# Attention on one core: the products that find the row maxima contract 32 rows instead of 96, two key blocks at once, and the score banks go by head

## The chip, the cores and the metric

The kernel runs on one core of a Trainium2 chip. The metric is the device time of one execution in microseconds (us); the fastest of repeated executions and their median lie close together. TensorE is the engine of the matrix products, VectorE (DVE), ScalarE (ACT) and GpSimd (POOL) work on elements, and SyncE (SP) issues the transfers that matter here. Products land in PSUM, which has 8 banks of 512 f32 numbers in each of 128 partitions.

## The reference

The program is two layers on 4096 tokens of 256 numbers (a gated delta rule with a mixture of experts, then a linear attention and a softmax attention, added). The change lies in the softmax attention alone, which has 8 heads of 32 numbers and no mask:

```python
attn = jnp.einsum('bhqd,bhkd->bhqk', q, k) * scale
attn = jax.nn.softmax(attn, axis=-1)
attn_out = jnp.einsum('bhqk,bhkd->bhqd', attn, v)
```

Softmax is the same whatever number is subtracted from all scores of a query. The kernel subtracts a maximum so that the exponentials stay in range; that maximum need not be exact.

## The kernel before

`phase_attention` is the last part of the program. Queries come in NB = 8 blocks of 512, heads in HP = 4 pairs, keys in NKT = 32 tiles of 128. One step is one key tile j for one pair p of one block b; n = 4b + p counts the pairs, and a pair has 32 steps. Everything is written out in order by hand and tied by semaphores.

Queries and keys are held as two f16 parts, high and low. `queries` has the high part in rows 0 to 31, the high part again in rows 32 to 63 and the low part in rows 64 to 95; `keys` has high, low, high. One product over these ROW = 96 rows gives high x high + high x low + low x high. Row 96 of the queries holds minus the maximum, and row 96 of the keys a constant, so that a product over KR = 97 rows gives the score less the maximum.

TensorE's order in a step is: the scores of tile j for both heads (L2127, four products of 64 key rows by 512 queries into `p_s[j % 2]`, two banks, one per head); then two maximum steps for a later pair (L2063, two products each, 64 queries by a block of 512 keys, into `p_m[k % 2]`, one bank); then the values of tile j-1 (L2082, f32, 64 columns for each head, into `p_o`). A product has a stationary side of 64 columns, so two products with outputs in partitions 0 to 63 and 64 to 127 use different columns of the array. An f32 product appears as two records.

The other engines follow. ScalarE takes the exponential of both heads in one instruction of 1024 elements (L2203) into `prob`, two deep. VectorE reduces each maximum bank of 512 to one column of `part_max` (L2221); 64 of them (NMAX = 2 heads x 4 query tiles x 8 key blocks) make a pair's maxima. `max_end` joins them, `max_rows` (L2072, eight small products with one column each) turns them into rows, and ScalarE copies these into row 96 of the queries (`copy_rows`, L2186). At step 1 ScalarE also copies the numerators of the pair before (`take_nums`, L2195), after VectorE has copied `p_o` (L2235). SyncE issues the query loads of the next block once a pair's scores are done. Ahead of the first step the 64 maximum steps of pair 0 and the first EARLY = 6 of pair 1 (12 products) run with nothing beside them.

The waits that the change touches are: the scores of step j wait for the exponentials of step j-2 (`exp_d`), the values of j-1 for those of j-1, a maximum product for the reduction two before it (`red_d`), and an activation for the scores of its step (`s_d`) and the values of step j-2 (`pv_d`).

Of the kernel before, what the change touches and what calls it, by code (L numbers as in the profile page):

```python
# [19 lines left out]
BLK = 512  # L20
# [19 lines left out]
DF = D // HF  # L40
# [3 lines left out]
SCORE_SCALE = D ** -0.5 / QK_SCALE ** 2  # L44
# [1807 lines left out]
def phase_attention(nc, g, ctx):  # L1852
# [5 lines left out]
    def sb(name, shape, dt=F32):  # L1858
        return ctx.enter_context(nc.sbuf_tensor(name, shape, dt))
# [3 lines left out]
    def sem(name):  # L1863
# [3 lines left out]
    HP = HF // 2  # L1867
    NKT = T // P
    KB = T // BLK
# [25 lines left out]
    part_max = sb("part_max", [P, 2 * SUB, KB])  # L1895
# [23 lines left out]

# [8 lines left out]
    LOADS = 6  # L1928
    READY = 3 * NB + sum(D >> (b * EX // NB) < D for b in range(NB)) + 2 * KC
    g.used_sems = sems  # L1930

# [7 lines left out]
        with looped(nc, engine, NB - 1) as i:  # L1939
            one(i + 1, i)  # L1940

    def max_steps(j):

        start = EARLY + 2 * j if j < MAX_END else 2 * (j - MAX_END)
        return range(start, start + 2)

    def max_step(k):

        hh, rest = divmod(k, NMAX // 2)
        return (hh,) + divmod(rest, KB)  # L1950

    block = ctx.enter_context(nc.Block())

    @block.sync
    def _(sp):
        def load_queries(b, p):
            for hh in range(2):
                c, at = place(2 * p + hh)
                for n, part in enumerate((0, 0, 1)):
                    sp.dma_start(queries[n * DF:(n + 1) * DF, p, hh, :],  # L1960
                                 g.parts_d[part * 2 * KC + c, at:at + DF, bass.ds(b * BLK, BLK)]).then_inc(q_in[p], 16)

        for p in range(HP):
            load_queries(0, p)
            for h in (2 * p, 2 * p + 1):
                c, at = place(h)
                for n, part in enumerate((0, 1, 0)):
                    sp.dma_start(keys[n * DF:(n + 1) * DF, h, :], g.parts_d[part * 2 * KC + KC + c, at:at + DF, 0:T]).then_inc(keys_in[p], 16)  # L1968
            if p == 0:
                for dst, src in ((lin_o[:], g.given["lin_o_t"].rearrange("(c p) n -> p c n", p=P)),  # L1970
                                 (nest_o[:], g.given["nest_o_t"].rearrange("(c p) n -> p c n", p=P)),
                                 (bias[:], g.given["lin_o_b"].partition_broadcast(P)), (nest_b[:], g.given["nest_o_b"].partition_broadcast(P))):
                    sp.dma_start(dst, src).then_inc(w_in, 16)

        def store(b):
            sp.wait_ge(out_d, b * SUB + SUB)
            sp.dma_start(g.out[bass.ds(b * BLK, BLK), :].rearrange("(s p) d -> p s d", p=P), out[:]).then_inc(out_out, 16)

        def one(b, before):

            sp.wait_ge(nums_d, b * KC)
            sp.dma_start(lin_q[:], g.lin_q_d[:, :, bass.ds(b * BLK, BLK)].rearrange("c p t -> p c t")).then_inc(lq_in, 16)
            for p in range(HP):

                sp.wait_ge(s_d, (b * HP + p + 1) * NKT)
# [66 lines left out]
    def _(pe):  # L2052
        te = nc.tensor

        def max_product(n, p, k):

            hh, sub, kb = max_step(k)

            if k >= 2 or not isinstance(n, int) or n > 0:
                pe.wait_ge(red_d, n * NMAX + (k - 1))  # L2060
            for x in range(2):
                at = sub * P + x * HALF
                last = te.matmul(p_m[k % 2][x * HALF:(x + 1) * HALF, :], queries[0:ROW, p, hh, at:at + HALF],  # L2063
                                 keys[0:ROW, 2 * p + hh, kb * BLK:(kb + 1) * BLK], start=True, stop=True)
            last.then_inc(mm_d, 1)

        def max_rows(n):
# [6 lines left out]
            last.then_inc(row_d, 1)  # L2074

        def values(n, p, j, hh):
            if hh == 0:
                if j == 0:

                    pe.wait_ge(o_d, n)  # L2080
# [18 lines left out]
            last.then_inc(fin_d, 1)  # L2099


        pe.wait_ge(q_in[0], 16 * LOADS)
        pe.wait_ge(keys_in[0], 16 * LOADS)
        for k in range(NMAX):
            max_product(0, 0, k)

        pe.wait_ge(cleared, 3)
        max_rows(0)
        pe.wait_ge(q_in[1], 16 * LOADS)
        pe.wait_ge(keys_in[1], 16 * LOADS)  # L2110
        for k in range(EARLY):
            max_product(1, 1, k)

        def one(b, before):
            for p in range(HP):
# [3 lines left out]

                pe.wait_ge(rowc_d, n * 2 + 2)  # L2120
                for j in range(NKT):

                    pe.wait_ge(exp_d, n * NKT + (j - 1) if before is not None or p > 0 or j > 0 else 0)
                    for hh in range(2):
                        for x in range(2):
                            at = j * P + x * HALF
                            last = te.matmul(p_s[j % 2][x * HALF:(x + 1) * HALF, hh, :], keys[0:KR, 2 * p + hh, at:at + HALF], queries[0:KR, p, hh, :],  # L2127
                                             start=True, stop=True)
                    last.then_inc(s_d, 1)
                    if j == MAX_END:  # L2130

                        pe.wait_ge(keys_in[nxt2], 16 * LOADS)
                        pe.wait_ge(q_in[nxt2], (b + 1) * (16 * LOADS) if p < HP - 2 else (b + 2) * (16 * LOADS))
# [46 lines left out]
    def _(act):  # L2180
# [16 lines left out]
        def one(b, before):  # L2197
            for p in range(HP):
                n = b * HP + p
                for j in range(NKT):  # L2200
                    act.wait_ge(pv_d, n * NKT + (j - 1) if before is not None or p > 0 or j > 0 else 0)
                    act.wait_ge(s_d, n * NKT + (j + 1))
                    a.activation(prob[:, j % 2], p_s[j % 2][:], ACT.Exp, scale=SCORE_SCALE).then_inc(exp_d, 1)  # L2203
                    if j == 1 and p > 0:
                        take_nums(b * HP + (p - 1))
                    elif j == 1 and before is not None:
                        take_nums(before * HP + (HP - 1))
                    if j == NKT - 2:
                        copy_rows(n + 1, (p + 1) % HP)
# [5 lines left out]
    def _(dve):  # L2215
        v = nc.vector

        def max_reduce(n, k):
            hh, sub, kb = max_step(k)
# [35 lines left out]
        def one(b, before):  # L2255
            for p in range(HP):
# [8 lines left out]
                for j in range(NKT):  # L2265
                    if j == MAX_END:
                        max_end(n + 1)
                    for k in max_steps(j):
                        max_reduce(n + 1 if j < MAX_END else n + 2, k)
# [165 lines left out]
```

## Time and profile before

| what | value |
|---|---|
| time, median of 3 | 4649.83 us (4649.33 to 4651.19) |
| span of the profiled execution | 4658.0 us |
| TensorE busy | 4395.0 us, 94% |
| VectorE busy | 3292.1 us, 71% |
| ScalarE busy | 1913.2 us, 41% |
| GpSimd busy | 1037.3 us, 22% |
| mean granted TensorE clock | 0.980 |

The profiled execution has no time of its own beside its span; the span is 8.2 us above the median of the timed runs. The first 2.69 ms are the other parts of the program, which the change leaves alone. In the profile "PE" is TensorE's products and "PEld" its loads of the stationary side. A product's duration contains the time in which it runs through the array, so that products started 0.22 us apart each last 0.38 us; what a product costs the stream is read from start to start.

### The profile page before, as it was taken

The numbers are of one execution on the slowest core, as the hardware profiler recorded it, in microseconds if no ns is written. First come the engines' busy times: TensorE is split into PE (matmuls) and PEld (weight loads), VectorE is DVE, ScalarE is ACT, GpSimd is POOL, SyncE is SP. The second block draws the span as 40 slices with busy tenths as digits, with TensorE's granted clock in tenths as the row PEclk, the third lists the DMA queues.
The fourth block names the chain that finished last, engine by engine and source line by source line (L and its number), as shares of the span: only waits on it lengthen the run. The fifth ranks groups of instructions, "written<-read, shape, count | busy, mean of one in ns | idle before, by whom it ended". The sixth has DMA issues, their size and how long they took to land. (4 is left out here: it accounts for less than half of the span.)

```text
span 4658.0 us, 151584 instructions
## 1 busy us (share of the span) xinstructions
PE 4395.0 (94%) x64527; PEld 2839.4 (61%) x64527; DVE 3292.1 (71%) x5448; ACT 1913.2 (41%) x2685; POOL 1037.3 (22%) x1042
## 2 busy tenths in 40 slices
PE   5999699999999999999968789999999999999998
PEld 4444499999999999996756624444444444444443
DVE  4899755655655655653459778787878888887876
ACT  2888411111111111110434426565655556565654
POOL 1000143343344344341047630000000000000000
PEclk9999899999999999999989979999999999999999
DMA  4544411111111111112344330000000000000000
GB/s 140 157 130 132 130 56 57 52 53 54 53 55 54 52 56 54 53 47 68 115 124 110 98 72 9 9 14 9 14 9 14 9 14 9 14 9 14 9 14 9
DMA packets 261652, 250.13 MB, mean 54 GB/s; under 512 B 51712, under 2 KB 230016, under 8 KB 260256
## 3 DMA queue, kind: packets, MB, share of 16 engines
q1 hardware_dynamic: 240528, 209.39, 15.0%
q0 software_dynamic: 6144, 16.79, 1.1%
q10 hardware_dynamic: 14352, 14.55, 0.9%
q8 instruction: 520, 8.52, 0.8%
q14 instruction: 108, 0.88, 0.1%
HBM read 135.27 MB, written 105.38 MB: 52 GB/s over the span
## 5 line engine op out<-in xcount | busy, mean ns | idle before, releaser
L2221 DVE TENSOR_REDUCE part_max<-p_m 128x1 f32<-128x512 f32 x2118 | 1364.1, 686 | 378.7 <-PE p_m L2063 371.2
L2203 ACT ACTIVATE prob<-p_s 128x1024 f32<-128x1024 f32 x1024 | 1047.8, 1023 | 749.2 <-PE p_s L2127 747.2
L2082 PE MATMUL p_o<-prob,v_one 128*64 128x512 f32 x4096 | 1054.4, 593 | 3.9 <-ACT prob L2203 0.5
L2063 PE MATMUL p_m<-keys,queries 96*64 96x512 f16 x4236 | 660.9, 387 | 27.9 <-DMA keys<-parts_d 20.3
L2127 PE MATMUL p_s<-queries,keys 97*64 97x512 f16 x4096 | 618.5, 380 | 0.0
L2127 PEld LDWEIGHTS p_s<-queries,keys 97*64 97x64 f16 x4096 | 227.1, 109 | 600.1 <-issue 594.6
L2063 PEld LDWEIGHTS p_m<-keys,queries 96*64 96x64 f16 x4236 | 238.2, 108 | 311.6 <-DVE part_max L2221 56.4
L848 PE MATMUL pd_pre<-inv,step 64*64 64x64 f32 x10240 | 384.4, 219 | 23.8 <-issue 22.1
L2031 POOL TENSOR_TENSOR attn<-o_num,o_inv 32x512 f32<-32x512 f32 x64 | 80.9, 1264 | 1458.5 <-DVE o_inv L2240 1452.0
L2082 PEld LDWEIGHTS p_o<-prob,v_one 128*64 128x64 f32 x4096 | 286.7, 136 | 163.7 <-issue 15.9
L848 PEld LDWEIGHTS pd_pre<-inv,step 64*64 64x64 f32 x10240 | 345.4, 135 | 57.4 <-issue 55.4
L590 PE MATMUL p_proj<-xn_t_all,proj_w_sb 128*128 128x512 f32 x768 | 337.7, 596 | 7.7 <-PEq L2366 7.7
L887 PE MATMUL pd_low<-step,inv 64*64 64x64 f32 x8192 | 304.6, 218 | 6.3 <-issue 3.4
L848 PE MATMUL pd_pre<-inv_low,upper 64*64 64x64 f32 x8192 | 295.0, 219 | 5.5 <-issue 5.5
L1087 DVE TENSOR_TENSOR step<-pd_pre,const 128x512 f32<-128x512 f32 x320 | 215.1, 688 | 105.9 <-PE pd_pre L848 105.9
L887 PEld LDWEIGHTS pd_low<-step,inv 64*64 64x64 f32 x8192 | 278.5, 135 | 10.3 <-issue 6.9
L848 PEld LDWEIGHTS pd_pre<-inv_low,upper 64*64 64x64 f32 x8192 | 273.1, 135 | 9.1 <-issue 6.9
L1091 DVE TENSOR_TENSOR inv_low<-low,pd_low 128x512 f32<-128x512 f32 x256 | 175.9, 687 | 132.8 <-PE pd_low L887 132.8
L590 PEld LDWEIGHTS p_proj<-xn_t_all,proj_w_sb 128*128 128x128 f32 x768 | 146.8, 191 | 193.0 <-issue 187.7
L1101 DVE TENSOR_TENSOR inv<-inv,pd_pre 128x512 f32<-128x512 f32 x256 | 176.1, 688 | 111.3 <-PE pd_pre L848 105.7
L1014 ACT ACTIVATE o_t<-pd_a 128x512 f32<-128x512 f32 x64 | 38.2, 597 | 494.6 <-PE pd_a L913 494.6
L999 ACT ACTIVATE rel<-diff 128x512 f32<-128x512 f32 x64 | 40.4, 631 | 467.4 <-DVE diff L1055 467.4
(245 smaller groups left out, 6612.8 us busy)
## 6 DMA issues: line engine op xcount, KB each, us to landing
q_d<-conv_q SPq DMA_DIRECT2D x16, 1024.0 KB, 5.0
v_d<-conv_v SPq DMA_DIRECT2D x16, 1024.0 KB, 5.0
k_d<-conv_k SPq DMA_DIRECT2D x16, 1024.0 KB, 6.5
sums<-sums_d SPq DMA_DIRECT2D x128, 128.0 KB, 3.0
k_t<-k_d SPq DMA_DIRECT2D x32, 512.0 KB, 4.6
q_t<-q_d SPq DMA_DIRECT2D x32, 512.0 KB, 3.4
v_t<-v_d SPq DMA_DIRECT2D x32, 512.0 KB, 3.4
slots_d<-zero ACTq DMA_DIRECT2D x1, 10112.0 KB, 32.5
```

The costliest lines, as they stand in the source:

```text
L590: last = te.matmul(p_proj[u % RING][:], g.proj_w_sb[:, n, c, p * P:(p + 1) * P], g.xn_t[:, c, b * BLK:(b + 1) * BLK], start=c == 0, stop=c ...
L848: last = te.matmul(out[hs, p, :], lhs(p, hs), rhs(p, hs), start=True, stop=True)
L887: last = te.matmul(p_low[x][hs, p, :], inv[x][hs, p, :], step[x][hs, p, :], start=k == 1 and p == 0, stop=k == NL - 1, skip_group_check=True)
L1087: v.tensor_tensor(step[x][:], p_pre[x][:], over_pairs(masks[:, k - 1, :]), ALU.mult).then_inc(step_d[x], 1)
L1091: v.tensor_tensor(inv_low[x][:], low_1[x][:], p_low[x][:], ALU.add).then_inc(lowc_d[x], 1)
L1101: v.tensor_tensor(inv[x][:] if k < NL else inv_fin[:, n.ring[x]], inv[x][:], p_pre[x][:], ALU.add).then_inc(up_d[x], 1)
L2031: po.tensor_tensor(attn[at:at + DF, c, :], o_num[DEN[hh], :], o_inv[DEN[hh], :], ALU.mult).then_inc(attn_d, 1)
L2063: last = te.matmul(p_m[k % 2][x * HALF:(x + 1) * HALF, :], queries[0:ROW, p, hh, at:at + HALF], keys[0:ROW, 2 * p + hh, kb * BLK:(kb + 1) ...
L2082: product = te.matmul(p_o[64 * hh:64 * hh + VW, :], g.v_one[:, j, p, hh:hh + 2, :].rearrange("p a d -> p (a d)"), prob[:, j % 2, hh, :], s ...
L2127: last = te.matmul(p_s[j % 2][x * HALF:(x + 1) * HALF, hh, :], keys[0:KR, 2 * p + hh, at:at + HALF], queries[0:KR, p, hh, :], start=True, ...
L2203: a.activation(prob[:, j % 2], p_s[j % 2][:], ACT.Exp, scale=SCORE_SCALE).then_inc(exp_d, 1)
L2221: v.tensor_reduce(part_max[:, hh * SUB + sub, kb:kb + 1], p_m[k % 2][:], AX.X, ALU.max).then_inc(red_d, 1)
```

## The change

The maximum products contract only the 32 high x high rows. The upper one reads rows 0 to 31 of `queries` and `keys`, the lower one rows 64 to 95 of `keys` (which hold the high part too) and of a new tile `queries_low`, whose rows 64 to 95 are loaded with the high part of the queries. In one step they take two key blocks of the same head and query tile, into the two banks of `p_m[k % 2]`. So there are NMAX = 32 maximum steps a pair, one in each step, four products each: two row groups by two halves of the columns. VectorE reduces the 1024 elements of both banks in one instruction.

The banks are shared out anew: `p_m` has two pairs of banks in place of two banks, and `p_s` two banks in place of two pairs, one for each head. So the scores of a head at step j wait for that head's exponential at step j-1. ScalarE has one activation of 512 elements for each head and step, and the counts of `s_d` and `exp_d` double. The two bias tiles move into `out`, to make room for `queries_low`.

```diff
-    NMAX = 2 * SUB * KB
+    NMAX = SUB * KB
     MAX_END = NKT - 3
-    EARLY = NMAX - 2 * MAX_END
+    EARLY = NMAX - MAX_END
+    UPPER = slice(0, DF)
+    LOWER = slice(2 * DF, 3 * DF)
...
+    queries_low = sb("queries_low", [P, HP, 2, BLK], F16)
...
-    bias = sb("bias", [P, D])
-    nest_b = sb("nest_b", [P, D])
...
-    p_s = [ctx.enter_context(nc.psum_tensor(f"p_s{n}", [P, 2, BLK], F32)) for n in range(2)]
-    p_m = [ctx.enter_context(nc.psum_tensor(f"p_m{n}", [P, BLK], F32)) for n in range(2)]
+    bias, nest_b = out[:, 0, :], out[:, 1, :]
+    p_s = [ctx.enter_context(nc.psum_tensor(f"p_s{n}", [P, BLK], F32)) for n in range(2)]
+    p_m = [ctx.enter_context(nc.psum_tensor(f"p_m{n}", [P, 2, BLK], F32)) for n in range(2)]
...
+                sp.dma_start(queries_low[LOWER, p, hh, :], g.parts_d[c, at:at + DF, bass.ds(b * BLK, BLK)]).then_inc(q_in[p], 16)
...
-                last = te.matmul(p_m[k % 2][x * HALF:(x + 1) * HALF, :], queries[0:ROW, p, hh, at:at + HALF],
-                                 keys[0:ROW, 2 * p + hh, kb * BLK:(kb + 1) * BLK], start=True, stop=True)
+                for half, (rows, side) in enumerate(((UPPER, queries), (LOWER, queries_low))):
+                    first = (2 * kb + half) * BLK
+                    last = te.matmul(p_m[k % 2][x * HALF:(x + 1) * HALF, half, :], side[rows, p, hh, at:at + HALF],
+                                     keys[rows, 2 * p + hh, first:first + BLK], start=True, stop=True)
...
-                pe.wait_ge(exp_d, n * NKT + (j + 1))
+            if hh == 0 and j == 0:
+                pe.wait_ge(o_d, n)
+            pe.wait_ge(exp_d, n * (2 * NKT) + (2 * j + hh + 1))
...
-                    pe.wait_ge(exp_d, n * NKT + (j - 1) if before is not None or p > 0 or j > 0 else 0)
                     for hh in range(2):
+                        if before is not None or p > 0 or j > 0:
+                            pe.wait_ge(exp_d, n * (2 * NKT) + (2 * j + hh - 1))
                         for x in range(2):
                             at = j * P + x * HALF
-                            last = te.matmul(p_s[j % 2][x * HALF:(x + 1) * HALF, hh, :], keys[0:KR, 2 * p + hh, at:at + HALF], queries[0:KR, p, hh, :],
+                            last = te.matmul(p_s[hh][x * HALF:(x + 1) * HALF, :], keys[0:KR, 2 * p + hh, at:at + HALF], queries[0:KR, p, hh, :],
                                              start=True, stop=True)
-                    last.then_inc(s_d, 1)
+                        last.then_inc(s_d, 1)
...
-                    for k in max_steps(j):
-                        max_product(n + 1 if j < MAX_END else n + 2, nxt if j < MAX_END else nxt2, k)
+                    max_products(n + 1 if j < MAX_END else n + 2, nxt if j < MAX_END else nxt2, max_step(j))
...
-                    act.wait_ge(s_d, n * NKT + (j + 1))
-                    a.activation(prob[:, j % 2], p_s[j % 2][:], ACT.Exp, scale=SCORE_SCALE).then_inc(exp_d, 1)
+                    for hh in range(2):
+                        act.wait_ge(s_d, n * (2 * NKT) + (2 * j + hh + 1))
+                        a.activation(prob[:, j % 2, hh], p_s[hh][:], ACT.Exp, scale=SCORE_SCALE).then_inc(exp_d, 1)
...
-            v.tensor_reduce(part_max[:, hh * SUB + sub, kb:kb + 1], p_m[k % 2][:], AX.X, ALU.max).then_inc(red_d, 1)
+            v.tensor_reduce(part_max[:, hh * SUB + sub, kb:kb + 1], p_m[k % 2][:].rearrange("p h t -> p (h t)"), AX.X, ALU.max).then_inc(red_d, 1)
```

On TensorE, a step in the middle of a pair and the scores of the next, before (`64x512` is the output; the number behind a name is that of the buffer):

```order
L2127 MATMUL p_s0<-queries,keys 64x512 x4
L2063 MATMUL p_m0<-keys,queries 64x512 x2
L2063 MATMUL p_m1<-keys,queries 64x512 x2
L2082 MATMUL p_o<-prob,v_one 64x512 x2
L2127 MATMUL p_s1<-queries,keys 64x512 x4
```

And the same place in the change:

```order
L2130 MATMUL p_s0<-queries,keys 64x512 x2
L2130 MATMUL p_s1<-queries,keys 64x512 x2
L2068 MATMUL p_m1<-keys,queries 64x512
L2068 MATMUL p_m1<-keys,queries_low 64x512
L2068 MATMUL p_m1<-keys,queries 64x512
L2068 MATMUL p_m1<-keys,queries_low 64x512
L2085 MATMUL p_o<-prob,v_one 64x512 x2
L2130 MATMUL p_s0<-queries,keys 64x512 x2
L2130 MATMUL p_s1<-queries,keys 64x512 x2
```

The number of products in a step is the same, 10. Between scores and values there now stand four maximum products with the same output buffer, alternately from `queries` and `queries_low`, and a step writes both score buffers where it wrote one.

On ScalarE, the end of a pair, where the row copies (`queries<-p_f`) stand, before:

```order
L2203 ACTIVATE prob<-p_s1 128x1024
L2203 ACTIVATE prob<-p_s0 128x1024
L2186 ACTIVATE queries<-p_f 1x512 x2
L2203 ACTIVATE prob<-p_s1 128x1024
L2203 ACTIVATE prob<-p_s0 128x1024
L2203 ACTIVATE prob<-p_s1 128x1024
L2195 ACTIVATE o_num<-o_raw 32x512 x2
```

And now:

```order
L2206 ACTIVATE prob<-p_s0 128x512
L2206 ACTIVATE prob<-p_s1 128x512
L2206 ACTIVATE prob<-p_s0 128x512
L2206 ACTIVATE prob<-p_s1 128x512
L2188 ACTIVATE queries<-p_f 1x512 x2
L2206 ACTIVATE prob<-p_s0 128x512
L2206 ACTIVATE prob<-p_s1 128x512
L2206 ACTIVATE prob<-p_s0 128x512
L2206 ACTIVATE prob<-p_s1 128x512
L2206 ACTIVATE prob<-p_s0 128x512
L2206 ACTIVATE prob<-p_s1 128x512
L2197 ACTIVATE o_num<-o_raw 32x512 x2
```

Each activation has become two, one per head; the two copies stand at the same place, now between the activations of step 30 and those of step 31, with two instructions of half the size for each step.

## Rows read from the trace of the kernel before

**Rows 1.** The page: busy time and share of each engine; chain by line.

```profile
PE 4395.0 (94%) x64527; PEld 2839.4 (61%) x64527; DVE 3292.1 (71%) x5448; ACT 1913.2 (41%) x2685; POOL 1037.3 (22%) x1042
...
PE p_o L2082 19%; PE p_m L2063 10%; PE p_s L2127 10%; DVE part_max L2221 1%; PE p_f L2095 1%; PE p_f L2097 1%; PE p_f L2157 0%; PE p_f L2162 0%; PE p_f L2072 0%; DMA keys<-parts_d 0%; DVE o_inv L2240 0%; SPq L1960 0%; SPq L1968 0%; DVE out_tile L2247 0%; ACT prob L2203 0%
```

**Rows 2.** One plain head pair: stretch, us, busy PE, PEld, DVE, ACT, POOL, clock, DMA.

```profile
3563.14:3619.18 56.04, 55.92 (x394) 24.15 (x392) 49.08 (x84) 35.18 (x37) 2.52 (x2) 1.00 0.02 5
```

**Rows 3.** The chain that ended last, one step: start us, us, what.

```profile
3504.26 0.86 PE p_o L2082 x4
3505.12 0.43 PE p_s L2127 x4
3505.55 0.43 PE p_m L2063 x4
```

**Rows 4.** Waits of the attention: who waited for whom, total us, times, longest.

```profile
ACT prob L2203 <- PE p_s L2127: 712.6, 897, 2.8
...
PEld p_m L2063 <- DVE part_max L2221: 14.5, 65, 0.5
```

**Rows 5.** Groups of instructions of the attention: busy us, mean ns of one, idle before.

```profile
L2221 DVE TENSOR_REDUCE part_max<-p_m 128x1 f32<-128x512 f32 x1962 | 1263.6, 686 | 333.2 <-PE p_m L2063 330.2
...
L2203 ACT ACTIVATE prob<-p_s 128x1024 f32<-128x1024 f32 x981 | 1003.8, 1023 | 714.5 <-PE p_s L2127 712.6
...
L2227 DVE TENSOR_REDUCE row_max<-part_max 128x8 f32<-128x64 f32 x31 | 6.8, 220 | 3.2
```

**Rows 6.** TensorE's timeline in the delta stage: start us, us, line, shapes, count.

```profile
1428.15 1.15 PE L848 MATMUL pd_pre<-inv,step 64*64 64x64 f32 x32
1429.23 0.44 PE L926 MATMUL pd_b<-wo,o_t 128*64 128x256 f32 x2
...
1430.80 0.39 PE L926 MATMUL pd_b<-wo,o_t 128*64 128x256 f32 x2
1431.11 1.15 PE L848 MATMUL pd_pre<-inv,step 64*64 64x64 f32 x32
1432.09 0.28 PE L848 MATMUL pd_pre<-k_t 64*64 64x64 f32 x4
```

**Rows 7.** TensorE's timeline at the end of a head pair.

```profile
3506.25 0.59 PE L2082 MATMUL p_o<-prob,v_one 128*64 128x512 f32 x2
3506.78 0.40 PE L2072 MATMUL p_f<-eye_h,neg_max 128*1 128x128 f16 x8
3507.11 0.41 PE L2127 MATMUL p_s<-queries,keys 97*64 97x512 f16 x2
...
3507.34 0.38 PE L2127 MATMUL p_s<-queries,keys 97*64 97x512 f16 x2
```

**Rows 8.** ScalarE: timeline at the end of a pair; a 128x512 activation elsewhere.

```profile
3507.23 1.20 ACT L2186 ACTIVATE queries<-p_f 1x512 f16<-1x512 f32 x2 [0.61 <-PE p_f L2072]
3508.46 1.02 ACT L2203 ACTIVATE prob<-p_s 128x1024 f32<-128x1024 f32 x1
...
L1014 ACT ACTIVATE o_t<-pd_a x64: 597/597/598, 593.7 to 2148.8; 128x512 f32<-128x512 f32 x64
```

**Rows 9.** TensorE's timeline in the second step of a pair.

```profile
3511.02 0.60 PE L2063 MATMUL p_m<-keys,queries 96*64 96x512 f16 x4
3511.73 0.65 PE L2082 MATMUL p_o<-prob,v_one 128*64 128x512 f32 x2
```

**Rows 10.** Timeline ahead of the first step: TensorE, then the DMA queue's issues.

```profile
2694.03 1.24 PE L2063 MATMUL p_m<-keys,queries 96*64 96x512 f16 x4 [0.19 <-DVE part_max L2221]
2695.45 0.64 PE L2063 MATMUL p_m<-keys,queries 96*64 96x512 f16 x2 [0.19 <-DVE part_max L2221]
...
2735.72 1.06 PE L2063 MATMUL p_m<-keys,queries 96*64 96x512 f16 x4
...
2739.60 0.64 PE L2127 MATMUL p_s<-queries,keys 97*64 97x512 f16 x2
...
2694.95 2.27 SPq L1960 DMA_DIRECT2D queries<-parts_d  x5
```

More of the change, by code:

```diff
@@ L1892, in phase_attention @@
     queries = sb("queries", [P, HP, 2, BLK], F16)
+    queries_low = sb("queries_low", [P, HP, 2, BLK], F16)
     eye_h = sb("eye_h", [P, P], F16)
     prob = sb("prob", [P, 2, 2, BLK])
-    part_max = sb("part_max", [P, 2 * SUB, KB])
+    part_max = sb("part_max", [P, 2 * SUB, KB // 2])
     row_max = sb("row_max", [P, 2 * SUB])
@@ L1927, in phase_attention @@
         sem(n) for n in ("lq_in", "base_in", "dens", "dene", "denr", "nums", "lin", "fin", "bb", "out", "out_out"))
-    LOADS = 6
+    KEY_LOADS = 6
+    QUERY_LOADS = 8
     READY = 3 * NB + sum(D >> (b * EX // NB) < D for b in range(NB)) + 2 * KC
@@ L1940, in blocks, with max_step, max_place @@
             one(i + 1, i)
[L1942 to L1947, printed above, removed]
+    def max_step(j):
+        return EARLY + j if j < MAX_END else j - MAX_END
+    def max_place(k):
         hh, rest = divmod(k, NMAX // 2)
-        return (hh,) + divmod(rest, KB)
+        return (hh,) + divmod(rest, KB // 2)
     block = ctx.enter_context(nc.Block())
@@ L1971, in _ @@
                                  (nest_o[:], g.given["nest_o_t"].rearrange("(c p) n -> p c n", p=P)),
-                                 (bias[:], g.given["lin_o_b"].partition_broadcast(P)), (nest_b[:], g.given["nest_o_b"].partition_broadcast(P))):
+                                 (bias, g.given["lin_o_b"].partition_broadcast(P)), (nest_b, g.given["nest_o_b"].partition_broadcast(P))):
                     sp.dma_start(dst, src).then_inc(w_in, 16)
@@ L1983, in one @@
             for p in range(HP):
-                sp.wait_ge(s_d, (b * HP + p + 1) * NKT)
+                sp.wait_ge(s_d, (b * HP + p + 1) * (2 * NKT))
                 load_queries(b + 1, p)
@@ L2053, in _, with max_products @@
         te = nc.tensor
-        def max_product(n, p, k):
-            hh, sub, kb = max_step(k)
+        def max_products(n, p, k):
+            hh, sub, kb = max_place(k)
             if k >= 2 or not isinstance(n, int) or n > 0:
@@ L2099, in final @@
             last.then_inc(fin_d, 1)
-        pe.wait_ge(q_in[0], 16 * LOADS)
-        pe.wait_ge(keys_in[0], 16 * LOADS)
+        pe.wait_ge(q_in[0], 16 * QUERY_LOADS)
+        pe.wait_ge(keys_in[0], 16 * KEY_LOADS)
         for k in range(NMAX):
-            max_product(0, 0, k)
+            max_products(0, 0, k)
         pe.wait_ge(cleared, 3)
         max_rows(0)
-        pe.wait_ge(q_in[1], 16 * LOADS)
-        pe.wait_ge(keys_in[1], 16 * LOADS)
+        pe.wait_ge(q_in[1], 16 * QUERY_LOADS)
+        pe.wait_ge(keys_in[1], 16 * KEY_LOADS)
         for k in range(EARLY):
-            max_product(1, 1, k)
+            max_products(1, 1, k)
         def one(b, before):
@@ L2121, in one @@
                 for j in range(NKT):
-                    pe.wait_ge(exp_d, n * NKT + (j - 1) if before is not None or p > 0 or j > 0 else 0)
                     for hh in range(2):
+                        if before is not None or p > 0 or j > 0:
+                            pe.wait_ge(exp_d, n * (2 * NKT) + (2 * j + hh - 1))
                         for x in range(2):
                             at = j * P + x * HALF
-                            last = te.matmul(p_s[j % 2][x * HALF:(x + 1) * HALF, hh, :], keys[0:KR, 2 * p + hh, at:at + HALF], queries[0:KR, p, hh, :],
+                            last = te.matmul(p_s[hh][x * HALF:(x + 1) * HALF, :], keys[0:KR, 2 * p + hh, at:at + HALF], queries[0:KR, p, hh, :],
                                              start=True, stop=True)
-                    last.then_inc(s_d, 1)
+                        last.then_inc(s_d, 1)
                     if j == MAX_END:
-                        pe.wait_ge(keys_in[nxt2], 16 * LOADS)
-                        pe.wait_ge(q_in[nxt2], (b + 1) * (16 * LOADS) if p < HP - 2 else (b + 2) * (16 * LOADS))
-                    for k in max_steps(j):
-                        max_product(n + 1 if j < MAX_END else n + 2, nxt if j < MAX_END else nxt2, k)
+                        pe.wait_ge(keys_in[nxt2], 16 * KEY_LOADS)
+                        pe.wait_ge(q_in[nxt2], (b + 1) * (16 * QUERY_LOADS) if p < HP - 2 else (b + 2) * (16 * QUERY_LOADS))
+                    max_products(n + 1 if j < MAX_END else n + 2, nxt if j < MAX_END else nxt2, max_step(j))
                     for hh in range(2):
@@ L2218, in max_reduce @@
         def max_reduce(n, k):
-            hh, sub, kb = max_step(k)
+            hh, sub, kb = max_place(k)
             dve.wait_ge(mm_d, n * NMAX + (k + 1))
-            v.tensor_reduce(part_max[:, hh * SUB + sub, kb:kb + 1], p_m[k % 2][:], AX.X, ALU.max).then_inc(red_d, 1)
+            v.tensor_reduce(part_max[:, hh * SUB + sub, kb:kb + 1], p_m[k % 2][:].rearrange("p h t -> p (h t)"), AX.X, ALU.max).then_inc(red_d, 1)
         def max_end(n):
@@ L2267, in one @@
                         max_end(n + 1)
-                    for k in max_steps(j):
-                        max_reduce(n + 1 if j < MAX_END else n + 2, k)
+                    max_reduce(n + 1 if j < MAX_END else n + 2, max_step(j))
                     if done is not None and j == 0:
```

3 lines of the change are left out of this document (removed).

## The prediction

> **What bounds the kernel now.** I read the page first. TensorE is busy for 94% of the span, and the chain that ended last has 19% in the value products (L2082), 10% in the maximum products (L2063) and 10% in the score products (L2127), nearly nothing on another engine [rows 1]. The change touches the attention alone, from about 2693 us on. It has 1024 steps (8 blocks x 4 head pairs x 32 key tiles); one plain head pair takes 56.04 us at a granted clock of 1.00 (2.4 GHz), in which VectorE is busy 49.08 and ScalarE 35.18 [rows 2]. In the chain a step is 0.43 us of scores, 0.43 of maximum products and 0.86 of values: 1.73 in all, without a gap [rows 3]. 32 x 1.73 is 55.3; the other 0.7 us of a pair are the row products (L2072) at the end and one wait on a VectorE copy. Who waits for whom agrees: ScalarE waits 712.6 us for scores, and TensorE's loads wait 14.5 us in all for the maximum reductions [rows 4]. So a step is worth what TensorE's own stream is worth; VectorE and ScalarE have room.
>
> **The change, part by part.**
>
> *Streaming.* Before, the four maximum products of a step are two couples; the halves of a couple lie in different columns of the array and run together, 0.216 us for 512 columns, so 0.43. Now the four lie in four separate pieces of 32 rows x 64 columns. If all four run together they stream for 0.216. That two products in different rows and columns run together is seen in the delta stage: 32 products of 64x64 take 0.98 us, 31 ns each, where a product of 64 columns in two passes streams 53 ns (an eighth of the 0.216 of 512, times two passes) [rows 6]. That two row groups over the *same* columns run together no row shows. Bounds: 0.216 saved, or nothing. I take 0.216: the outputs are in different banks, and nothing in the rows ties a product to its column neighbours. Per step: -0.216.
>
> *Changing the shape of the pieces.* This is the cost that the diff does not name. Scores (97 rows) and values (128) use the whole height of the array; the new products use a quarter of it. The trace has such changes. In the delta stage a batch of 32 64x64 products takes 0.98 us to the next batch of the same shape, and 1.08 to products of 128x64 [rows 6]: 0.10 lost. The first couple after a change also lasts 0.44 against 0.39 for a later one [rows 6], 0.05, as its weights could not be loaded ahead. The reverse change, from products at 1430.80 to 1431.11, is 0.31 where a couple takes 0.216: 0.10 again. In the attention the row products show the same with f16: values at 3506.25 stream 0.43, the next starts at 3506.78, 0.10 late; and the first scores after it last 0.41, the next 0.38, so the load costs 0.02-0.03 with f16 weights [rows 7]. Now each step has two such changes: scores to maximum products (0.095 + 0.024, and 0.012 for four starts), and back to values (0.095 + 0.051, f32 weights). Sum +0.277 a step. With the streaming: +0.061 a step, step 1.79, x 1024 = **+62 us**.
>
> The Trainium skill (TensorEngine Tiling, Key Properties) states that changing the tiling mode, not just the tile, drains TensorE; by that alone the gap would be expected here, and the trace agrees with its 0.10 us at every such change.
>
> *Activations.* One of 1024 elements (1023 ns) becomes two of 512; the same shape on ScalarE takes 597 ns elsewhere [rows 5, 8]. So 1.20 us a step, under 1.79. But the score banks are now one per head, and scores of step j+1 wait for the activation of step j, not j-1. A signal takes some 0.05: the row products end at 3507.18, the copy starts at 3507.23 [rows 7, 8]. Timed from a step's first score, whose product lasts 0.38, the first head's activation ends at 0.43 + 0.60 = 1.03, the second's at 1.63; the second head's next scores may start at 1.68 and are due at 1.79 + 0.22 = 2.01. Slack 0.33: no wait in a plain step. Cover is gone where ScalarE has something else in its queue, twice a pair. (a) At the end of a pair it copies two rows, 1.20 us, starting 0.12 after the step's scores, and activations begin 1.35 after them [rows 7, 8]. Before, the double banks hide this. Now activations end at 1.95 and 2.55; scores due at 1.79 start at 2.00 (0.21 late), those then due at 2.22 start at 2.60 (0.38 late). What is queued behind them on TensorE, the maximum products and values, moves with them. (b) After step 1 it copies the numerators, two instructions again: about 0.1 late, as the steps before have built up slack. Against it, the values of step 1 wait 0.28 for VectorE's copy of the output (0.71 from products to values where 0.43 is usual [rows 9]); with a longer step and a shorter reduction ahead of that copy I make it 0.2, so -0.1. Net +0.6 a pair, x 32 = **+19 us**.
>
> *Reductions.* 512 elements take 686 ns, 64 take 220 [rows 5]: 1.04 ns an element, so 1024 take 1.22 us. A step has one in place of two (2 x 0.686, less a little overlap). VectorE gets lighter; it held TensorE for almost nothing in the steps, so nothing is won there.
>
> *Before the first step.* 64 reductions with TensorE waiting for each go at 1.42 per two [rows 10], 45.5 us; 32 of 1.24 are 39.7: -5.8. The 12 products ahead of the first step take 3.88 [rows 10]; three double ones need some 2.6: -1.3. Two more query loads stand ahead of the keys on the queue, at 2.27 / 5 = 0.45 us each [rows 10]: +0.9. Together **-6 us**. Later query loads are two more per pair, issued a full block ahead of use: nothing. The bias tiles that move into the output tile are read before its first write: nothing.
>
> **The sum**: +62 + 19 - 6 = +75 us on the profiled span of 4658.0, and the same difference on the median of 4649.83, which is 8 us lower: **4725 us**, slower by 1.6%. (0.2%, 9 us, is about what a measurement here tells from no change.)
>
> **Rivals.**
> - *Faster: no gap between shapes.* If the change between whole-height and 32-row pieces cost nothing (the rows show other pairs of shapes, never this one), a step would be 1.51. The waits on ScalarE would grow to about 1.3 us a pair more than before, as its slack shrinks to 0.05: -0.216 x 1024 + 42 - 6 = -186, 4464 us. Against it stands that every change seen, in rows or in columns, costs 0.10. It decides at 0.19: if both changes with their loads cost less than that a step, instead of 0.277, the kernel is faster. 5%. The Trainium skill (TensorE: Matmul & The Clock Gate, Measured speedup vs the span model) has row-packed products starting about 4 ns apart and four at 3.07 times the speed; applied alone to this kernel it would be this rival, but it says nothing there of products of another shape in between.
> - *Half of it*: one of the two changes is hidden, as the 32-row weights load beside the scores. Step 1.727 - 0.216 + 0.146 = 1.657; with waits of some +25 us, 4650 - 72 + 25 - 6, about 4597. 5%.
> - *The row groups run one after the other* (one port for what streams in, or the same columns collide). Then the gaps come and nothing is saved: 0.216 x 1024 more, less the ScalarE waits that the longer step covers (17): 4927 us. Nothing in the trace speaks for or against it but the diagonal pieces of [rows 6]. 9%.
> - *A chain over ScalarE in every step*: activation or semaphores take longer than I have, and the single bank per head becomes the bound. Each 0.1 beyond the 0.33 of slack is 102 us: near 4820. The 597 ns speaks against it. 5%.
> - *No change of time*, where gaps and streaming just cancel: 2%.
> - My forecast: 74%, with its own range 4695 to 4755 (gap 0.09 to 0.11, load 0.02 to 0.06, stalls a pair 0.2 to 1.1).
>
> **Numbers.** Slower by over 0.2%: 74 + 9 + 5 = 88%. Faster: 10%. Same: 2%. The range goes from 4670 to 4800: it holds the likeliest case whole and reaches some way to the ScalarE chain; it leaves out the serial row groups, both faster rivals and the tail of the rest, a little under 2 in 10.
>
> **What would show it.** In the changed trace: four maximum products within some 20 ns of each other; a start 0.31 after the last couple of scores and values about 0.35 after the first maximum product; step 1.79 by the chain; clock still 1.00; a plain pair near 58.5 us; longer steps at the turn of a pair, where TensorE's loads wait for the activation. It is wrong if the step is 1.51 (no gap), 1.66 (one gap) or 2.0 (serial), or if the loads of scores wait for ScalarE in every step.

## The result, and the profile after

The changed kernel takes 4703.77 us (4700.84 to 4710.49) against 4650.51 us (4649.33 to 4652.89): the ratio is 1.0113, with a 95% interval of 1.0101 to 1.0125. It is slower by 53 us, where 75 were forecast, and the time lies in the range.

The page of the profile after, TensorE's share and the chain by line; they answer to [rows 1]:

```profile
PE 4430.8 (94%) x64527; PEld 2637.8 (56%) x64527; DVE 3232.6 (69%) x4389; ACT 1976.6 (42%) x3709; POOL 1037.1 (22%) x1042
...
PE p_o L2085 21%; PE p_s L2130 9%; PE p_m L2068 7%; DVE part_max L2224 1%; PE p_f L2098 1%; ACT prob L2206 1%; PE p_f L2100 1%; DVE o_raw L2238 0%; PE p_f L2159 0%; PE p_f L2164 0%; ACT queries L2188 0%; PE p_f L2077 0%; DMA keys<-parts_d 0%; SPq L1962 0%; SPq L1971 0%
```

TensorE is as busy as before, 94% of a longer span; the maximum products have fallen from 10% of the chain to 7% and the values have risen from 19% to 21%, although no value product was changed. One plain head pair of the profile after (stretch, its length, then busy time of TensorE's products and loads, VectorE, ScalarE, GpSimd, clock and DMA), as [rows 2]:

```profile
3578.03:3636.18 58.15, 57.88 (x393) 17.50 (x393) 47.44 (x52) 37.16 (x69) 2.54 (x2) 1.00 0.02 6
```

58.15 us in place of 56.04, at the same clock of 1.00. VectorE's work has fallen, ScalarE's risen by 2 us; neither fills the pair. The score products of the whole attention (count, shortest/median/longest duration in ns, first and last start):

```profile
L2130 PE MATMUL p_s<-queries,keys x4096: 376/381/637, 2720.4 to 4676.8; 97*64 97x512 f16 x196
```

From the first to the last score there are 1956.4 us. In the profile before, the same view has 2739.6 and 4630.1, that is 1890.5. The steps alone have cost 65.9 us. TensorE's timeline of one plain step of the change (start us, duration us, line, shapes, count):

```profile
3559.57 0.60 PE L2130 MATMUL p_s<-queries,keys 97*64 97x512 f16 x4
3560.10 0.40 PE L2068 MATMUL p_m<-keys,queries 32*64 32x512 f16 x1
3560.11 0.40 PE L2068 MATMUL p_m<-keys,queries_low 32*64 32x512 f16 x1
3560.11 0.40 PE L2068 MATMUL p_m<-keys,queries 32*64 32x512 f16 x1
3560.11 0.40 PE L2068 MATMUL p_m<-keys,queries_low 32*64 32x512 f16 x1
3560.44 1.08 PE L2085 MATMUL p_o<-prob,v_one 128*64 128x512 f32 x4
3561.35 0.60 PE L2130 MATMUL p_s<-queries,keys 97*64 97x512 f16 x4
```

The four maximum products start within 0.01 us of each other. From scores to maximum products there are 0.53 us, where two couples of scores stream 0.43: 0.10 of gap. From there to the values 0.34, where 512 columns stream 0.216: a gap again and the load. From values to the next scores 0.91, where [rows 3] has 0.86: the first value products had no weights loaded ahead, their loads start with them at 3560.44 (in the kernel before, 0.21 us ahead of them). Together 1.78 in place of 1.73.

Where the time went, by the two profiles:

| stretch | before | after | difference |
|---|---|---|---|
| first query load issued to first maximum product | 12.0 | 13.0 | +1.0 |
| first maximum product to first score | 51.3 | 40.7 | -10.6 |
| first to last score | 1890.5 | 1956.4 | +65.9 |
| last score to the end | 27.8 | 25.9 | -1.9 |

That is +54.4, against +53.3 between the medians. The span differs by 44.7 only, because the profiled execution of before spent 9.6 us more in the stages ahead of the attention, which are the same in both kernels.

### The profile page after: what moved, and what is told of

It reads as the page before. It is cut to its first block and busy times, and to the rows that moved or that the text cites. A ratio compares the mean times of both kernels' runs of the same rounds, so it can differ in the third digit from the quotient of the medians.

```text
span 4702.7 us, 152544 instructions
## 1 busy us (share of the span) xinstructions
PE 4430.8 (94%) x64527; PEld 2637.8 (56%) x64527; DVE 3232.6 (69%) x4389; ACT 1976.6 (42%) x3709; POOL 1037.1 (22%) x1042
## 5 line engine op out<-in xcount | busy, mean ns | idle before, releaser
L2224 DVE TENSOR_REDUCE part_max<-p_m 128x1 f32<-128x1024 f32 x1059 | 1293.5, 1224 | 493.8 <-PE p_m L2068 462.1
L2206 ACT ACTIVATE prob<-p_s 128x512 f32<-128x512 f32 x2048 | 1111.4, 595 | 743.5 <-PE p_s L2130 741.8
L2085 PE MATMUL p_o<-prob,v_one 128*64 128x512 f32 x4096 | 1106.9, 618 | 4.7 <-DVE o_raw L2238 0.2
L2068 PE MATMUL p_m<-keys,queries 32*64 32x512 f16 x2118 | 437.0, 406 | 37.4 <-DMA keys<-parts_d 21.4
L2068 PE MATMUL p_m<-keys,queries_low 32*64 32x512 f16 x2118 | 436.9, 406 | 0.0
L2068 PEld LDWEIGHTS p_m<-keys,queries 32*64 32x64 f16 x2118 | 114.8, 102 | 466.6 <-DVE part_max L2224 393.2
L2085 PEld LDWEIGHTS p_o<-prob,v_one 128*64 128x64 f32 x4096 | 202.8, 135 | 241.0 <-issue 219.1
```

The lines of the kernel that those rows point to most:

```text
L2068: last = te.matmul(p_m[k % 2][x * HALF:(x + 1) * HALF, half, :], side[rows, p, hh, at:at + HALF], keys[rows, 2 * p + hh, first:first + BLK ...
L2206: a.activation(prob[:, j % 2, hh], p_s[hh][:], ACT.Exp, scale=SCORE_SCALE).then_inc(exp_d, 1)
```

## The experiments

Each kernel ran in rounds with the kernel before on the same chip; ratios are to it. The time of the kernel before differed between the chips (4650.5, 4657.1, 4618.5, 4621.1 us), so the last column, taken from each profile by the view of the score products, compares better from chip to chip: it was 1956.4 and 1956.1 us in the two profiles of the change.

| run | median us | ratio, 95% interval | first to last score us |
|---|---|---|---|
| the change | 4703.77 | 1.0113 (1.0101 to 1.0125) | 1956.4 |
| e1_banks_only | 4666.34 | 1.0017 (1.0008 to 1.0027) | 1907.4 |
| e2_one_row_group | 4972.96 | 1.0681 (1.0661 to 1.0700) | 2216.3 |
| e3_tiny_between | 4903.48 | 1.0526 (1.0505 to 1.0546) | 2142.3 |
| e4_every_second | 4613.52 | 0.9913 (0.9896 to 0.9929) | 1856.3 |
| e5_rows_on_vector | 4663.15 | 1.0094 (1.0077 to 1.0111) | 1945.8 |
| e6_second_rows_vector | 4575.91 | 0.9909 (0.9892 to 0.9926) | 1858.8 |
| e7_second_no_act_copies | 4572.51 | 0.9906 (0.9890 to 0.9923) | 1857.0 |
| e8_change_again | 4669.45 | 1.0108 (1.0091 to 1.0125) | 1956.1 |
| e9_second_nums_pool | 4564.16 | 0.9873 (0.9856 to 0.9889) | 1845.5 |

**e1_banks_only: the banks and activations without the new products.**

```diff
-            for x in range(2):
-                at = sub * P + x * HALF
-                for half, (rows, side) in enumerate(((UPPER, queries), (LOWER, queries_low))):
-                    first = (2 * kb + half) * BLK
-                    last = te.matmul(p_m[k % 2][x * HALF:(x + 1) * HALF, half, :], side[rows, p, hh, at:at + HALF],
-                                     keys[rows, 2 * p + hh, first:first + BLK], start=True, stop=True)
+            for half in range(2):
+                first = (2 * kb + half) * BLK
+                for x in range(2):
+                    at = sub * P + x * HALF
+                    last = te.matmul(p_m[k % 2][x * HALF:(x + 1) * HALF, half, :], queries[0:ROW, p, hh, at:at + HALF],
+                                     keys[0:ROW, 2 * p + hh, first:first + BLK], start=True, stop=True)
```

> The change with its maximum products back at the whole height (96 rows, four products in two couples); banks by head, two activations a step and one reduction of 1024 stay. Theory (the loss comes from the two changes of tile shape in each step, 0.27 us, against 0.216 saved; the banks cost only the turn of a pair): a plain step of 1.73 us; at the turn of a pair the scores wait about 0.5 us for ScalarE, and the wait at step 1 stays near 0.3: +16 us; ahead of the first step -10; so about 4655 us (4648 to 4668). Rival (single score banks and twice the activations are what the change pays for): steps well over 1.73, total near 4700 or more.

Measured: 1.0017, within its theory: 9 us over the kernel before in the same rounds, and 49 us less than the change between first and last score. The chain that ended last, one step of it (start us, us, what):

```profile
3601.07 0.43 PE p_s L2130 x4
3601.51 0.43 PE p_m L2068 x4
3601.94 0.86 PE p_o L2085 x4
```

A plain step is the 1.73 of before, with the single score banks, two activations a step and one reduction. So these do not bind a plain step. What they cost is at the turn of a pair: 1907.4 against 1890.5, 17 us. The rest of the change's loss in the steps, 49 us, comes with the 32-row products.

**e2_one_row_group: the four products in the same rows.** All four read `queries` and `keys` in rows 0 to 31.

```diff
-                for half, (rows, side) in enumerate(((UPPER, queries), (LOWER, queries_low))):
+                for half, (rows, side) in enumerate(((UPPER, queries), (UPPER, queries))):
```

> The change, but all four maximum products of a step read rows 0 to 31 (the same values), so the two products of a column half have the same piece of the array and must follow each other. Theory (two row groups over the same columns do run together and save 0.216 us a step): the section from maximum products to values grows from 0.34 to 0.55 us, step 2.00, and the ScalarE wait at the turn shrinks a little: 4704 + 221 - 7, about 4917 us. Rival (the four were already limited by something that they share, as one port or the start of the values): less than 100 us more.

Measured: 4973 us, and the steps take 260 us more than in the change. Two causes. A plain step went from 1.78 to 1.99, as expected (0.21): the second couple does have to wait when it shares its rows, so in the change the two row groups over the same columns really run at once. A plain pair takes 64.52 in place of 58.15, which makes 204 us for 32 pairs; it is less than 0.21 for every step, as the longer step covers waits at the turn of a pair. The other 56 us were not expected. Two stretches of this run, in the first head pair and later (length, busy TensorE, loads, VectorE, ScalarE, GpSimd, clock, DMA):

```profile
2740.00:2850.00 110.00, 110.00 (x360) 24.86 (x358) 35.87 (x31) 32.65 (x60) 0.00 (x0) 0.50 0.01 2
3000.00:3064.00 64.00, 63.92 (x385) 18.05 (x384) 43.03 (x43) 36.38 (x67) 2.52 (x2) 1.00 0.05 13
```

The first head pair ran at a granted clock of 0.50 (1.2 GHz) throughout, with TensorE busy 110.00 of 110.00 us, and took 119 us, where the change's 60.6 and the 6.4 more of a later pair make 67. The clock rose 10 us into the second pair, which took 4 us too long. All the other kernels had 2.4 GHz within 9 us of the first score. That is the missing 56 us, and it was there in all four timed executions: their mean granted clock is 0.969 or 0.970, that of every other kernel 0.978 to 0.982.

**e3_tiny_between: a change of shape that saves nothing.** In e1_banks_only, one line more ahead of the maximum products:

```diff
+            te.matmul(p_m[k % 2][0:HALF, 0, 0:8], queries[UPPER, p, hh, 0:HALF], keys[UPPER, 2 * p + hh, 0:8], start=True, stop=True)
```

> The kernel of e1_banks_only with one tiny product more in each step: 32 rows, 64 columns, 8 elements, put between the scores and the maximum products; its result is overwritten at once. It saves nothing and streams 3 ns, but changes the tile shape twice. Theory (each change of shape costs a gap of 0.095 us and the exposed load of the next weights, whatever is computed): +0.24 to +0.33 us a step over e1_banks_only, so 4655 + 245 to 340, about 4900 to 4990 us. Rival (no price on the change of shape; the 0.28 us seen belong to the four products with short columns or to the two streams at once): within 30 us of e1_banks_only.

Measured: 4903 us, 237 more than e1_banks_only in the same rounds, 235 in the steps: 0.23 us for each of the 1024. The rival is out. TensorE's timeline of one step:

```profile
3804.73 0.39 PE L2131 MATMUL p_s<-queries,keys 97*64 97x512 f16 x2
3805.05 0.19 PE L2064 MATMUL p_m<-keys,queries 32*64 32x8 f16 x1
3805.17 0.62 PE L2069 MATMUL p_m<-keys,queries 96*64 96x512 f16 x4
3805.62 1.03 PE L2086 MATMUL p_o<-prob,v_one 128*64 128x512 f32 x4
3806.49 0.60 PE L2131 MATMUL p_s<-queries,keys 97*64 97x512 f16 x4
```

The tiny product starts 0.32 after the last couple of scores, which streams 0.22: 0.10 gap. The maximum products follow 0.12 later, though the tiny one streams 8 columns. They last 0.62, two couples, against 0.60 for scores: 0.02 of load. The products that pay are ordinary 96-row products, so the price belongs to the change of shape and not to what is computed in 32 rows. A tiny product of 96 rows, one more product without a change of shape, was not tested. In e4_every_second, below, a second group of the same shape starts 0.24 after the first, which streams 0.216; by that a further product and its load would cost some 0.02, an estimate, and not 0.23.

**e4_every_second: half as many changes.** The maximum products of two steps stand together in the odd one, the reductions too.

```diff
-                    max_products(n + 1 if j < MAX_END else n + 2, nxt if j < MAX_END else nxt2, max_step(j))
+                    for i in ((j - 1, j) if j % 2 == 1 else ()):
...
+                        max_products(n + 1 if i < MAX_END else n + 2, nxt if i < MAX_END else nxt2, max_step(i))
...
-                    max_reduce(n + 1 if j < MAX_END else n + 2, max_step(j))
+                    for i in ((j - 1, j) if j % 2 == 1 else ()):
+                        if i == MAX_END:
+                            max_end(n + 1)
+                        max_reduce(n + 1 if i < MAX_END else n + 2, max_step(i))
```

> The change with the maximum products of two steps issued together in every second (odd) step, so half as many changes of shape; the rest is as it was. Theory (a separate section of maximum products costs 0.48 us, a joined one only 0.216 more): -0.265 us for two steps, 136 us in all; but the steps without maximum products are only 1.29 us long, and the second head's scores then wait for its activation some 0.06 to 0.1 us (single banks), +30 to +50. So 4704 - 136 + 40, about 4608 us (4585 to 4635), faster than the kernel before. Rival (VectorE, busy for 2.95 of every 3.3 us and now fed in bursts, becomes the bound, or the score banks do): 4650 us or more.

Measured: 0.9913, faster than the kernel before by 44 us in the same rounds, and 100 us less than the change in the steps. TensorE's timeline of a step with eight maximum products and the start of one without:

```profile
3504.12 0.68 PE L2130 MATMUL p_s<-queries,keys 97*64 97x512 f16 x4
3504.72 0.40 PE L2068 MATMUL p_m<-keys,queries 32*64 32x512 f16 x1
...
3504.96 0.37 PE L2068 MATMUL p_m<-keys,queries 32*64 32x512 f16 x1
...
3505.28 1.08 PE L2085 MATMUL p_o<-prob,v_one 128*64 128x512 f32 x4
3506.19 0.60 PE L2130 MATMUL p_s<-queries,keys 97*64 97x512 f16 x4
3506.62 0.60 PE L2085 MATMUL p_o<-prob,v_one 128*64 128x512 f32 x2
```

From 3504.72 the first four, at 3504.96 the next four, 0.24 later and without a gap, then one change back to the values. The step lasts 2.07 and the one without 1.30, together 3.37 where the change has 3.56. The gain is 0.19 for two steps and not 0.265: the scores last 0.68 here against 0.60, because the second head's have to wait for its activation in the short step ahead of them (it ends at 3504.33, they start at 3504.39, 0.27 after the first head's). That was the expected price of the single banks.

**e5_rows_on_vector: the row copies off ScalarE.** In the change, `copy_rows` goes from ScalarE to VectorE.

```diff
-                    if j == NKT - 2:
-                        copy_rows(n + 1, (p + 1) % HP)
...
+        def copy_rows(n, p):
+            dve.wait_ge(row_d, n + 1)
+            for hh in range(2):
+                v.tensor_copy(queries[ROW:KR, p, hh, :], p_f[ROW_AT[hh]:ROW_AT[hh] + 1, :]).then_inc(rowc_d, 1)
```

> The change with the two row copies at the end of a pair on VectorE in place of ScalarE. Theory (those copies stand ahead of the activations that the single score banks wait for, which costs 0.22 us in step 31 and 0.29 in step 0 of each pair): step 31 back to 1.80, step 0 back to 1.78, 0.49 to 0.51 x 32 = -16 us, ratio to the kernel before 1.0113 - 0.0034 = 1.008. Rival (the turn is slow for another reason, as the row products or the wait for the copied rows themselves): no difference, or slower, as VectorE gets 1.2 us more a pair.

Measured: 1.0094 beside 1.0108 for the change in the same rounds, intervals that overlap; by the steps -10.3 us. The steps at the turn did fall to 1.80 and 1.78. But in the pairs p = 2 and p = 3 of each block step 1 rose from 2.00 to 2.31. TensorE's timeline there, then VectorE's:

```profile
3549.09 0.40 PE L2068 MATMUL p_m<-keys,queries 32*64 32x512 f16 x1
...
3549.96 1.08 PE L2085 MATMUL p_o<-prob,v_one 128*64 128x512 f32 x4 [0.46 <-DVE o_raw L2241]
...
3545.11 1.42 DVE L2235 CAST queries<-p_f 1x512 f16<-1x512 f32 x2
3546.56 1.22 DVE L2222 TENSOR_REDUCE part_max<-p_m 128x1 f32<-128x1024 f32 x1
3547.70 0.54 DVE L2294 RECIPROCAL den<-den 128x64 f32<-128x64 f32 x1
3548.16 1.16 DVE L2222 TENSOR_REDUCE part_max<-p_m 128x1 f32<-128x1024 f32 x1
3549.24 0.67 DVE L2241 COPY o_raw<-p_o 128x512 f32<-128x512 f32 x1
```

The two copies take VectorE 1.42 us; the reductions of steps 31 and 0 and a reciprocal of `den` stand behind them, so the copy of the output (L2241) starts at 3549.24, and TensorE's values wait for it until 3549.96, 0.87 after the maximum products, where the same step of the change has 0.56 and a plain step 0.34. The turn gained 0.49 us in each of 32 pairs, 16 us; 0.31 in 16 of them, 5 us, were given back through another engine's queue.

**e6_second_rows_vector: the same in e4_every_second.**

> e4_every_second and the row copies on VectorE together. Theory: step 0 of a pair there takes 1.58 against 1.30, and that 0.28 goes: -9 us, ratio 0.9913 - 0.0019 = 0.989. Rival: VectorE, at 49 of 54 us a pair, is now late for the next joined products, and the gain is lost: ratio 0.991 or above.

Measured: 0.9909, no difference from e4_every_second, and 2.5 us more in the steps. The rival came true: step 0 fell to 1.30, but step 1 of the pairs p = 2 and p = 3 rose to 2.91 from 1.99.

**e7_second_no_act_copies: and the numerators on GpSimd.** The two activations of `take_nums` become products with a column of ones on GpSimd, at the head of `normalise`.

```diff
+                po.tensor_tensor(o_num[DEN[hh], :], o_raw[NUM[hh], :], spread(one_col[NUM[hh], :], [DF, BLK]), ALU.mult).then_inc(num_d, 1)
```

> e6 with the numerator copies moved from ScalarE to GpSimd, so that ScalarE does nothing but activations. Theory: the steps 2 and 3 of a pair, 1.49 and 2.29 in e4_every_second against 1.30 and 2.07, lose their 0.41: -13 us more, ratio about 0.986. Rival: the 0.41 come from VectorE's copy of the output and not from ScalarE: no difference from e6.

Measured: 0.9906, 1.8 us less in the steps than e6. The expected 13 us did not come: in e6 the steps 2 and 3 were no longer late in most pairs (1.30 and 2.08 for p = 2, 1.49 and 2.29 in e4), since step 1, late for VectorE, had given ScalarE the time. Only step 3 of the first pair of each block was left to win, 2.24 to 2.07. So this run could not decide between theory and rival.

**e9_second_nums_pool: only the numerators moved.** It is e4_every_second with the edit of e7, and the row copies on ScalarE.

> e4_every_second with the numerator copies on GpSimd, and the row copies left on ScalarE (VectorE has nothing more than there). Theory (what ScalarE has in its queue beside the activations costs 0.41 us a pair in steps 2 and 3; the row copies cost 0.28 in step 0): steps 2 and 3 at 1.30 and 2.07, step 0 still 1.58, a plain pair 54.4 in place of 54.83, the whole stretch of steps 1856 - 13 = 1843 us, ratio 0.9913 - 0.0028 = 0.9885. Rival (the 0.41 are VectorE's): steps 2 and 3 as in e4_every_second, no difference.

Measured: 0.9873 (0.9856 to 0.9889), 57 us under the kernel before in the same rounds. The score products of the whole attention:

```profile
L2135 PE MATMUL p_s<-queries,keys x4096: 376/381/637, 2693.6 to 4539.1; 97*64 97x512 f16 x196
```

1845.5 us from first to last score, 10.8 less than e4_every_second. Steps 2 and 3 are 1.30 and 2.07, step 0 is still 1.58, a plain pair 54.41. The 0.41 us were ScalarE's. They come in three pairs of four, as the pair p = 1 was not late there (1.32 and 2.07 in both), so it is 10.8 and not 13. This version has the lowest ratio measured, faster than both kernels.

**e8_change_again: the change, in the rounds of e5 to e7.**

> The change itself once more, on the same chip and in the same rounds as e5 to e7, to measure them against: ratio to the kernel before 1.0113 as on record, within 0.002.

Measured: 1.0108, and the steps agree with the first profile within 0.3 us.

## Why the prediction was right

**The gap and the loads** (forecast +0.061 us a step, +62 us): right in kind and nearly in size. A plain step is 1.782 against 1.728, 0.054 x 1024 = 55 us. Its parts stood as forecast: a gap of 0.10 on the way in, 0.34 from maximum products to values (about 0.35 forecast), 0.05 at the first value products. e3_tiny_between prices the two changes at 0.23 a step with nothing saved, e1_banks_only shows that without them the step is 1.73, and e4_every_second that half as many give back 100 us. The rivals with no gap (1.51) or with one (1.66) are out. The rival of a chain over ScalarE in every step is out by e1_banks_only, whose step of 1.73 is shorter still.

**The streaming** (-0.216 a step): right. The rival that row groups over the same columns run one after the other is out: the four starts lie within 0.01 us, and e2_one_row_group, which makes them share rows, costs 0.21 more. That rival was priced rightly: 221 less 17 of waits, and e2's later pairs cost 204. (By its own terms the prediction's 4927 should read 4929.)

**ScalarE at the turn of a pair** (forecast +19 us): the mechanism was right, the term mis-sized. A plain pair has 2.11 us more than before, of which 32 x 0.054 are the steps; 0.38 is left, 12 us for 32 pairs. TensorE's timeline at the end of a pair and ScalarE's:

```profile
3634.18 0.62 PE L2130 MATMUL p_s<-queries,keys 97*64 97x512 f16 x4
...
3635.07 1.08 PE L2085 MATMUL p_o<-prob,v_one 128*64 128x512 f32 x4
3636.18 0.89 PE L2130 MATMUL p_s<-queries,keys 97*64 97x512 f16 x4
3637.00 0.40 PE L2068 MATMUL p_m<-keys,queries 32*64 32x512 f16 x1
...
3634.30 1.20 ACT L2188 ACTIVATE queries<-p_f 1x512 f16<-1x512 f32 x2 [0.82 <-PE p_f L2077]
3635.53 2.18 ACT L2206 ACTIVATE prob<-p_s 128x512 f32<-128x512 f32 x4
```

The copies start 0.12 after the scores and take 1.20, as in [rows 8]. The next scores start 2.00 after 3634.18, due at 1.80: 0.20 late, 0.21 were forecast. Then the second head's: four scores last 0.89 in place of 0.60, 0.29 late, where 0.38 were forecast, because ScalarE's four activations take 2.18 and not 2.40. A pair of them takes 1.09: each lasts 597 ns or a little less, and the second starts 0.49 after the first. The 0.1 forecast after step 1 did not come (steps 2 and 3 are 1.78); that the quicker activations are why was not tested. The step that failed in size is "the first head's activation ends at 0.43 + 0.60 = 1.03, the second's at 1.63": it is about 1.52. ScalarE's timeline of two plain steps shows it:

```profile
3596.77 1.08 ACT L2206 ACTIVATE prob<-p_s 128x512 f32<-128x512 f32 x2 [0.70 <-PE p_s L2130]
3598.55 1.09 ACT L2206 ACTIVATE prob<-p_s 128x512 f32<-128x512 f32 x2 [0.70 <-PE p_s L2130]
```

**A sign that misled.** The prediction said that it would be wrong if the loads of scores waited for ScalarE in every step. The view of waits says just that (engine and line, waited for: total us, times, longest):

```profile
PEld p_s L2130 <- ACT prob L2206: 562.4, 1800, 0.9
...
PEld p_o L2085 <- DVE o_raw L2238: 13.8, 31, 0.4
```

1800 waits, and yet no loss. In the view of [rows 4], of the kernel before, the same loads are idle about as long, with no other engine named that they waited for:

```profile
PEld p_s L2127 <- issue: 569.1, 1838, 0.8
```

The two activations that start at 3596.77 end 1.08 later, at 3597.85. The next ones start at 3598.55, 0.42 after the scores that they read (the step began at 3598.13), and the second head's scores start 0.22 into the step, at 3598.35: half a microsecond after their bank was free. Their load starts at 3598.13, with the first head's products, 0.27 after the semaphore; so it waits for its turn on TensorE, and the view names the semaphore that came last. The chain and e1_banks_only decide, not this row: that run has the same waits (569.7 us in 1803) and the plain step of before.

**Ahead of the first step** (forecast -6 us): -9.6. The loads cost +1.0 (forecast +0.9). TensorE's timeline there:

```profile
2685.12 0.63 PE L2068 MATMUL p_m<-keys,queries 32*64 32x512 f16 x1 [0.49 <-DVE part_max L2224]
...
2686.25 0.63 PE L2068 MATMUL p_m<-keys,queries 32*64 32x512 f16 x1 [0.49 <-DVE part_max L2224]
...
2717.91 0.63 PE L2068 MATMUL p_m<-keys,queries 32*64 32x512 f16 x1
...
2720.45 1.07 PE L2130 MATMUL p_s<-queries,keys 97*64 97x512 f16 x4
```

The double reductions go at 1.13 us and not at 1.24, since two of them overlap by a tenth of a microsecond, too; 32 of them are 36.2 us (39.7 forecast). From 2717.91 to the first score there are 2.54 (2.6 forecast). Two smaller things were not in the forecast: VectorE's lighter load did win 0.26 us in step 7 of the second pair of each block (2.04 to 1.78), where "nothing is won there" was said (2 us in all), and the end is 1.9 us shorter, for which the runs give no cause.

So the sum is 55 + 12 - 2 - 10 - 2 = 53 us, where the forecast had 62 + 19 - 6. Each of the three terms came out lower than forecast, which makes the forecast 22 us too high; no error hid another.

## What to carry to other kernels

Smaller pieces of the array are worth their streaming time only where products of the same shape stand together: here a step that goes to another shape and back pays 0.27 us with the loads of weights, more than the 0.216 that four-way packing saved, and joining two such groups turned a loss of 1.1% into a gain of 0.9%. Look for such pairs in the trace of before, as the time from start to start across a change of shape. When a buffer loses its second copy, look for the one place where its reader has something else in its queue, and before moving that work to another engine, see what stands behind it there.

## What the runs showed of the hardware that was not expected

- In e2_one_row_group the granted clock stayed at 0.50 after the first score, with TensorE busy without a break; in the change, whose steps differ only in that the four maximum products run at once, it was 1.00 from 8 us after the first score. Ahead of it both had been at 0.50 in the same way. In e2_one_row_group it rose 129 us after the first score, as the first two products with 128 rows and 128 columns since then (L2159, 2.08 us for both) ended; that is the order of events and no shown cause. Whether it was the serial 32-row products that kept the clock down was not tested; it cost 56 us in each execution.
- Activations of 512 elements last 597 ns each, but two in a row take 1.09 us and four 2.18: about 0.1 us of each second one is hidden. Reductions of 1024 elements last 1.21 us and start 1.13 apart when in a row.
- The row copy of 1 partition by 512 elements takes VectorE 0.71 us (1.42 for two) and ScalarE 0.60 (1.20).
- The gap at the change from 97 rows to 32 was the same 0.10 us with products of 512 columns and with one of 8 behind it. On the way back it was 0.12, load of the weights included: 0.34 less 0.216 in the change, and 0.12 behind the tiny product of e3_tiny_between.
